# Cross attention: probabilities turned by VectorE in blocks of 32 by 32 and placed through DRAM, image sums two steps behind, text in a stage of its own

## The chip, the cores and the metric

The kernel runs on one core of a Trainium2 chip. The metric is the device time of one execution in microseconds, the median of three runs. A profile of one further execution gives the span and the rows below.

## The reference, cut to what matters

The program is a two-layer perceiver block: 16 batches of 64 latents of width 256 attend to a context of 1601 rows. The change is in the cross attention of the second layer (16 heads of 64, inner width 1024). Its keys and values have two parts: the first 77 context rows (text) with weights of their own, and the other 1524 (image). Each part has its own softmax, and the two results are added.

```python
def _attend(q, k, v):
    sim = jnp.einsum('bihd,bjhd->bhij', q, k) * SCALE
    attn = jax.nn.softmax(sim, axis=-1)
    out = jnp.einsum('bhij,bjhd->bihd', attn, v)
...
# text:  k = ctx[:, :77] @ Wk,     v = ctx[:, :77] @ Wv
# image: k = ctx[:, 77:] @ Wk_ip,  v = ctx[:, 77:] @ Wv_ip
# x = x + (attend(q, text) + attend(q, image)) @ Wo + bo
```

(The last three lines are a summary, with x normalised before it is projected to q.)

## The kernel before, in words

The program is a row of stages, each with its own block of engine programs: load, norm, positions, the first layer's local attention (near_attention or far_attention), self attention, a mixture of experts, then norm and cross_attention, a scan and a second mixture.

cross_attention goes over 8 tiles of 128 tokens (two batches each). A tile has 16 steps: 2 batches x 8 pairs of heads. A step handles one batch's 64 tokens for two heads, 128 rows of scores. Image keys and values are never formed: key_side multiplies the queries by the key weights (a, 128 x 256), scores multiplies a by the transposed context ct (3 x 508 columns), sums multiplies the turned probabilities by the context rows cn, and value_side applies the value weights to the turned result. Precision is kept by splitting: a, ct, cn and the turned probabilities are each held as a high part in fp32r and a low part (the rest), and three products are added.

In step n, TensorE does in this order: text scores of n (L2151); the twelve transposes of the probabilities of n - 1 (turn, L2169) into PSUM; the scores of n (18 matmuls, L2159 to L2161); the transpose of the text probabilities (L2176); the transpose of the sums of n - 2 (L2190); key_side for n + 1 (L2145); the sums of n - 1 (24 matmuls, L2182 of 512 columns and L2183 of 256); value_side of n - 2 (L2201, L2203). ScalarE copies the turned probabilities out of PSUM as high part (pt_hi, L2302), then does the exponentials of n (L2365 image, L2368 text). VectorE subtracts for the low part (pt_lo, L2308), takes the maxima of the scores (L2417, L2418), makes the bias (L2421), scales the text probabilities (L2410) and joins the two halves of the sums (L2432, L2435).

The text keys and values are made inside the steps, for the next tile or batch (L2127: keys, 3 uses of a PSUM bank per tile; L2136: values, 4 uses per tile). At tile borders TensorE also makes the queries (L2117) and the output projection (L2213). GpSimd splits the context, 8 pieces per batch (L1907, L1909), which SyncE loads one at a time into one buffer, staged (L1900, L2032). It runs ahead of the steps, as far as the two sets of buffers allow. The order on each engine is written out by hand; waits are on semaphores, and every engine runs its queue in order. The positions of the first layer go through DRAM: load_positions issues 32 small DMAs (L303) in near_attention.

## Time and profile before

| | |
|---|---|
| median of 3 runs | 2578.5 us (2574.81 to 2583.28) |
| the profiled execution | 2586.37 us, its span 2584.0 us |
| TensorE matmuls busy | 2328.9 us (90%), weight loads 1821.4 |
| VectorE, ScalarE, GpSimd busy | 1314.9 (51%), 957.4 (37%), 856.9 (33%) us |
| bytes moved | 141.32 MB, mean 55 GB/s |

The span is the time from the first to the last instruction in the trace; the profiled execution's own time is 2.4 us longer. An engine's busy time counts its own instructions alone, so a waiting engine shows as idle. A matmul's time in the trace overlaps the next one's, so its cost is read from the distance between starts.

### The profile page before, as it was taken

What the parts mean: (1) busy time and instruction counts of PE and PEld (TensorE: products, weight loads), DVE (VectorE), ACT (ScalarE), POOL (GpSimd) and SP (SyncE); (2) the same over time, 40 slices, a digit from 0 to 9 for tenths busy, and PEclk for the clock granted to TensorE, in tenths of its full rate; (3) what the DMA queues carried; (4) which work ended last, traced back from release to release, by engine and by line L of the source; (5) the groups of instructions that cost most, each with busy time, mean ns of one, the idle gap of its engine ahead of it and who ended that gap; (6) DMA issues with size and microseconds to landing.
All of it is one profiled execution on the core that took longest, in us unless ns stands there. A gap on an engine that the chain in (4) does not pass through costs nothing. (4 is left out here: it accounts for less than half of the span.)

```text
span 2584.0 us, 35941 instructions
## 1 busy us (share of the span) xinstructions
PE 2328.9 (90%) x13845; PEld 1821.4 (70%) x13845; DVE 1314.9 (51%) x2478; ACT 957.4 (37%) x2031; POOL 856.9 (33%) x534
## 2 busy tenths in 40 slices
PE   3787759949999999999999999999999998687896
PEld 2454445647888888888888888888888886234673
DVE  4897533344544544544544544544444444695543
ACT  2564121123443433443443443443343443452330
POOL 2563215225414314314224224233232100262444
PEclk8898869979999999999999999999999998798898
DMA  4100063122112102102002001111111003101372
GB/s 102 17 11 5 1 232 113 35 90 58 44 35 62 37 29 68 31 14 89 25 19 82 27 25 60 44 31 54 50 32 54 13 1 156 57 0 41 109 143 88
DMA packets 69927, 141.32 MB, mean 55 GB/s; under 512 B 24912, under 2 KB 42576, under 8 KB 65408
## 3 DMA queue, kind: packets, MB, share of 16 engines
q1 hardware_dynamic: 62992, 120.50, 14.8%
q0 software_dynamic: 6768, 18.49, 3.1%
q8 instruction: 117, 1.92, 0.3%
q14 instruction: 50, 0.41, 0.1%
HBM read 124.21 MB, written 14.75 MB: 54 GB/s over the span
## 5 line engine op out<-in xcount | busy, mean ns | idle before, releaser
L2182 PE MATMUL img_ps<-cn,pt_hi 127*128 127x512 f32 x1536 | 551.2, 400 | 10.4 <-POOL cn L1909 10.3
L2183 PE MATMUL img_ps<-cn,pt_lo 127*128 127x256 f32 x1536 | 430.0, 280 | 0.0
L1907 POOL TENSOR_SCALAR ct<-staged 128x762 fp32r<-128x762 f32 x64 | 136.1, 2127 | 755.5 <-DMA staged<-in_ctx_t 523.8
L2182 PEld LDWEIGHTS img_ps<-cn,pt_hi 127*128 127x128 f32 x1536 | 289.7, 189 | 70.2 <-POOL cn L1909 10.5
L2159 PE MATMUL s_ps<-ct,a_hi 128*128 128x508 f32 x768 | 312.3, 407 | 0.0
L2308 DVE TENSOR_TENSOR pt_lo<-t_ps,pt_hi 127x512 fp32r<-127x512 f32 x384 | 241.4, 684 | 135.1 <-ACT pt_hi L2302 135.1
L2161 PE MATMUL s_ps<-ct,a_lo 128*128 128x508 f32 x768 | 301.6, 393 | 0.0
L2160 PE MATMUL s_ps<-ct,a_hi 128*128 128x508 f32 x768 | 301.5, 393 | 0.0
L2183 PEld LDWEIGHTS img_ps<-cn,pt_lo 127*128 127x128 f32 x1536 | 289.4, 188 | 0.0
L2365 ACT ACTIVATE prob<-s_ps,bias 128x1524 f32<-128x1524 f32 x128 | 196.5, 1535 | 141.4 <-DVE bias L2421 141.4
L2302 ACT ACTIVATE pt_hi<-t_ps 127x512 fp32r<-127x512 f32 x384 | 202.0, 599 | 80.8 <-PE t_ps L2169 76.9
L2418 DVE TENSOR_REDUCE top<-s_ps 128x1 f32<-128x1524 f32 x128 | 222.0, 1735 | 0.0
L2432 DVE TENSOR_SCALAR o_part<-img_ps,inv 128x256 f32<-128x256 f32 x128 | 61.9, 484 | 307.1 <-PE img_ps L2183 307.1
L1907 POOL TENSOR_SCALAR cn<-staged 128x768 fp32r<-128x768 f32 x64 | 136.6, 2134 | 230.4 <-DMA staged<-in_ctx_n 183.1
L2332 ACT ACTIVATE pt_txt<-t_ps 77x128 f32<-77x128 f32 x128 | 34.9, 273 | 453.5 <-PE t_ps L2176 453.5
L2169 PE MATMUL t_ps<-small,prob 128*127 128x128 f32 x1536 | 196.9, 278 | 0.0
L2417 DVE TENSOR_REDUCE top<-s_ps 128x1 f32<-128x77 f32 x128 | 30.4, 238 | 321.9 <-PE s_ps L2161 321.9
L2169 PEld LDWEIGHTS t_ps<-small,prob 128*127 128x127 f32 x1536 | 180.7, 191 | 0.1
L2161 PEld LDWEIGHTS s_ps<-ct,a_lo 128*128 128x128 f32 x768 | 144.7, 188 | 31.9
L2160 PEld LDWEIGHTS s_ps<-ct,a_hi 128*128 128x128 f32 x768 | 145.6, 190 | 27.4
L2159 PEld LDWEIGHTS s_ps<-ct,a_hi 128*128 128x128 f32 x768 | 144.9, 189 | 27.2
L1632 PE MATMUL up_ps_b<-up_all_m,xt_b 128*128 x436 | 152.9, 483 | 1.5 <-issue 0.8
(369 smaller groups left out, 3929.4 us busy)
## 6 DMA issues: line engine op xcount, KB each, us to landing
staged<-in_ctx_n SPq DMA_DIRECT2D x64, 384.0 KB, 3.1
staged<-in_ctx_t SPq DMA_DIRECT2D x64, 381.0 KB, 3.2
up_all_m<-in_up SPq DMA_DIRECT2D x8, 2048.0 KB, 13.0
down_all_m<-in_down SPq DMA_DIRECT2D x8, 1024.0 KB, 27.1
sums_m<-y_b SPq DMA_DIRECT2D x63, 128.0 KB
w_shared<-in_wq SPq DMA_DIRECT2D x7, 1024.0 KB, 5.5
w_shared<-in_wo SPq DMA_DIRECT2D x7, 1024.0 KB, 4.9
win<-in_ctx_near SPq DMA_DIRECT2D x16, 128.0 KB, 2.0
```

Source lines behind the costliest of these rows:

```text
L1632: last = nc.tensor.matmul(up_ps[j % 2][:, own], xt[j % 2][:, c, :], m.up[:, bass.ds(expert, 1), c, own].rearrange("p a h -> p (a h)"), sta ...
L1907: nc.gpsimd.tensor_scalar(hi, piece, 1.0, None, ALU.mult).then_inc(first.hi_done, 1)
L2159: nc.tensor.matmul(out, a_hi[:, c, :], ct[b][:, 0, c, cols], start=c == 0, stop=False)
L2160: nc.tensor.matmul(out, a_hi[:, c, :], ct[b][:, 1, c, cols], start=False, stop=False)
L2161: last = nc.tensor.matmul(out, a_lo[:, c, :], ct[b][:, 0, c, cols], start=False, stop=c == C - 1)
L2169: last = nc.tensor.transpose(t_ps[bank][0:IBLK, j * P:(j + 1) * P], prob[:, at:at + IBLK], k.ident)
L2182: nc.tensor.matmul(img_ps[:], pt_hi[0:IBLK, j, :], rows[0:IBLK, :, j, :], start=j == 0, stop=False)
L2183: last = nc.tensor.matmul(img_ps[:, D:2 * D], pt_lo[0:IBLK, j, :], rows[0:IBLK, 0, j, :], start=False, stop=j == IB - 1)
L2302: nc.scalar.activation(out, t_ps[bank][0:rows, 0:cols], ACT.Copy).then_inc(hi_kept, 1)
L2308: nc.vector.tensor_tensor(out, t_ps[bank][0:rows, 0:cols], hi.bitcast(F32), ALU.subtract).then_inc(t_kept[bank], 1)
L2365: nc.scalar.activation(prob[:, TXT:M].rearrange("p (j m) -> p j m", j=SB), s_ps[:, 1:4, 0:SBLK], ACT.Exp, bias=bias[s][:, 1:2], scale=SCAL ...
L2418: nc.vector.tensor_reduce(top[s][:, 1:2], s_ps[:, 1:4, 0:SBLK], mybir.AxisListType.XY, ALU.max).then_inc(topped, 1)
```

## The change

The twelve transposes of a step leave TensorE. VectorE turns the image probabilities in blocks of 32 by 32, in four instructions (128 x 384) as soon as the image exponential is done. SyncE stores each result (192 KB) to DRAM and, when it has landed, loads it back into 32 partitions in the order that the sums need: four stores and four loads a step. ScalarE and VectorE split what came back (moved, in SBUF) into pt_hi and pt_lo in two halves of 128 x 768 each, where before they read PSUM in three parts of 127 x 512. The sums run two steps behind the scores instead of one, in blocks of 128 context rows instead of 127, as 36 matmuls of 256 columns into one half of the bank, so that VectorE needs one instruction on the sums instead of two. One context piece is loaded in each step, behind the step's eight DMAs. The loops over tiles are unrolled.

text_stage, new, stands between the positions stage and the local attention: it makes all text keys (24 uses of a bank) and values (20 uses), stores them to DRAM, and cross_attention loads them tile by tile. load_positions moves into it from near_attention and far_attention.

```diff
+            load_positions(sp, k)
+            for p in range(PAIRS1):
+                wait_kept(sp, len(K_COLS) * (p + 1))
+                sp.dma_start(k.k_txt[:, :, p, :].rearrange("i q n -> q i n"),
+                             keys[p % KEYS][:].rearrange("q (i n) -> q i n", i=NT)).then_inc(keys_out[p % KEYS], 16)
...
+                for c in range(C):
+                    if kind == "k":
+                        last = nc.tensor.matmul(out[:, 0:cols.stop - cols.start], w.wk[:, c, at * P:(at + 1) * P],
+                                                w.text[:, c, cols], start=c == 0, stop=c == C - 1)
+                    else:
+                        last = nc.tensor.matmul(out[0:rows_of(at), :], w.text[:, c, at * P:at * P + rows_of(at)],
+                                                w.wv[:, c, cols], start=c == 0, stop=c == C - 1)
+                last.then_inc(done, 1)
...
-        load_positions(sp, k)
...
-        prob = sb("prob1", [P, M])
+        prob = sb("prob1", [P, TXT + IB * P])
+        blocks = sb("prob_blocks", [P, Q, IB, QR])
+        block_rows = nc.dram_tensor("prob_rows", (2, Q, P, RUN), F32).ap()
+        moved = [sb(f"prob_moved{s}", [P, Q, IB, QR]) for s in range(2)]
...
+            for g in range(N):
+                s, (i, b, p, n) = g % 2, parts(g)
+                if g >= 2:
+                    sp.wait_ge(moved_in[s], 16 * Q * (g // 2))
+                for m in range(Q):
+                    sp.wait_ge(turned, Q * g + m + 1)
+                    sp.dma_start(block_rows[s, m], blocks[:, m].rearrange("p j r -> p (j r)")).then_inc(stored[m], 16)
+                if g >= 2:
+                    sp.wait_ge(split_done, 2 * (g - 1))
+                for m in range(Q):
+                    sp.wait_ge(stored[m], 16 * (g + 1))
+                    sp.dma_start(moved[s][m * QR:(m + 1) * QR].rearrange("c a j r -> c a (j r)"),
+                                 block_rows[s, m].rearrange("(a c) f -> c a f", a=Q)).then_inc(moved_in[s], 16)
+                if g // PAIRS1 + 1 < NB:
+                    load(g // PAIRS1 + 1, g % PAIRS1)
...
-            def sums(n):
-                rows = cn[n // PAIRS1]
-                for j in range(IB):
-                    nc.tensor.matmul(img_ps[:], pt_hi[0:IBLK, j, :], rows[0:IBLK, :, j, :], start=j == 0, stop=False)
-                    last = nc.tensor.matmul(img_ps[:, D:2 * D], pt_lo[0:IBLK, j, :], rows[0:IBLK, 0, j, :],
-                                            start=False, stop=j == IB - 1)
-                last.then_inc(summed, 1)
+            def sums(g):
+                rows = cn[g // PAIRS1 % 2]
+                if g % PAIRS1 == 0:
+                    pe.wait_ge(cn_split, 4 * (g // PAIRS1) + 4)
+                if g:
+                    pe.wait_ge(sums_kept, g)
+                for h in range(2):
+                    pe.wait_ge(split_done, 2 * g + h + 1)
+                    for j in range(IB)[half(h)]:
+                        n = min(P, IMG - j * P)
+                        for at, (left, right) in enumerate(((pt_hi, 0), (pt_hi, 1), (pt_lo, 0))):
+                            last = nc.tensor.matmul(img_ps[:, 0:D], left[0:n, j, :], rows[0:n, right, j, :],
+                                                    start=j == 0 and at == 0, stop=j == IB - 1 and at == 2)
...
+            for g in range(N + 3):
+                if g < N:
+                    if g:
+                        pe.wait_ge(exp_done, g)
+                    kept(a_place)
+                    text_scores(g)
+                    scores(g)
+                if 1 <= g <= N:
+                    turn_text(g - 1)
+                if g >= 3:
...
+                if 2 <= g <= N + 1:
+                    sums(g - 2)
...
+                if 1 <= g <= N:
+                    act.wait_ge(moved_in[(g - 1) % 2], 16 * Q * ((g - 1) // 2 + 1))
+                    for h in range(2):
+                        if g >= 2:
+                            act.wait_ge(summed if h else half_summed, g - 1)
+                        nc.scalar.activation(in_quarters(pt_hi, h), by_block(moved[(g - 1) % 2], h),
+                                             ACT.Copy).then_inc(pt_hi_kept, 1)
...
+                    dve.wait_ge(image_exp, g + 1)
+                    source = prob[:, TXT:].rearrange("p (j m c) -> p m j c", j=IB, m=Q)
+                    for m in range(Q):
+                        if g:
+                            dve.wait_ge(stored[m], 16 * g)
+                        nc.vector.transpose(blocks[:, m], source[:, m]).then_inc(turned, 1)
...
+                if 1 <= g <= N:
+                    for h in range(2):
+                        dve.wait_ge(pt_hi_kept, 2 * (g - 1) + h + 1)
+                        nc.vector.tensor_tensor(in_quarters(pt_lo, h), by_block(moved[(g - 1) % 2], h),
+                                                in_quarters(pt_hi, h).bitcast(F32), ALU.subtract).then_inc(split_done, 1)
+                if 2 <= g <= N + 1:
+                    dve.wait_ge(summed, g - 1)
+                    nc.vector.tensor_scalar(o[:], img_ps[:, 0:D], inv[(g - 2) % 3][:, 1:2], None,
+                                            ALU.mult).then_inc(sums_kept, 1)
```

## Rows read from the trace of the kernel before

**Rows 1.** Busy time in stretches: length, us and (instructions) per engine, TensorE's clock, DMA share, GB/s.
```profile
1442.73:1454.06 11.33, 11.33 (x79) 9.76 (x75) 5.57 (x12) 4.71 (x11) 0.00 (x0) 1.00 0.00 1
595.27:2143.60 1548.33, 1545.74 (x10164) 1317.39 (x10164) 742.92 (x1400) 625.87 (x1440) 466.83 (x239) 1.00 0.14 41
```
**Rows 2.** Timeline of an ordinary step on TensorE: start us, duration us.
```profile
1442.75 0.45 PE L2151 MATMUL s_ps<-k_txt,q 128*128 128x77 f32 x2
1443.03 1.54 PE L2169 MATMUL t_ps<-small,prob 128*127 128x128 f32 x12
1444.32 0.47 PE L2159 MATMUL s_ps<-ct,a_hi 128*128 128x508 f32 x1
...
1448.54 0.27 PE L2176 MATMUL t_ps<-small,prob 128*77 128x128 f32 x1
...
1449.23 0.48 PE L2182 MATMUL img_ps<-cn,pt_hi 127*128 127x512 f32 x1
...
1453.37 0.28 PE L2183 MATMUL img_ps<-cn,pt_lo 127*128 127x256 f32 x1
...
1454.08 0.45 PE L2151 MATMUL s_ps<-k_txt,q 128*128 128x77 f32 x2
```
**Rows 3.** Timeline of the same step on VectorE and ScalarE.
```profile
1450.67 0.17 DVE L2421 TENSOR_SCALAR bias<-top 128x2 f32<-128x2 f32 x1
...
1450.87 1.53 ACT L2365 ACTIVATE prob<-s_ps,bias 128x1524 f32<-128x1524 f32 x1 [0.97 <-DVE bias L2421]
...
1452.60 0.20 ACT L2368 ACTIVATION_READ_ACCUMULATOR prob<-s_ps,bias 128x1 f32 x1
```
**Rows 4.** The page's costliest groups: busy us, mean ns of one, idle before.
```profile
L2308 DVE TENSOR_TENSOR pt_lo<-t_ps,pt_hi 127x512 fp32r<-127x512 f32 x384 | 241.4, 684 | 135.1 <-ACT pt_hi L2302 135.1
...
L2302 ACT ACTIVATE pt_hi<-t_ps 127x512 fp32r<-127x512 f32 x384 | 202.0, 599 | 80.8 <-PE t_ps L2169 76.9
```
**Rows 5.** Single lines of the code: duration ns min/median/max, first and last start us.
```profile
L739 DVE TENSOR_TENSOR share<-tent,marks x32: 1214/1484/1755, 69.4 to 241.3; 128x1536 f32<-128x1536 f32 x16, 128x1024 f32<-128x1024 f32 x16
...
L2421 DVE TENSOR_SCALAR bias<-top x128: 169/170/1553, 567.1 to 2151.8; 128x2 f32<-128x2 f32 x128
...
L2410 DVE TENSOR_SCALAR prob<-prob,inv x128: 261/264/1894, 569.5 to 2155.4; 128x77 f32<-128x77 f32 x128
...
L1907 POOL TENSOR_SCALAR cn<-staged x64: 2127/2134/2192, 561.1 to 2017.7; 128x768 fp32r<-128x768 f32 x64
```
**Rows 6.** Timeline of SyncE's queue: two DMAs issued one after the other.
```profile
40.82 0.81 SPq L345 DMA_DIRECT2D pos_rows<-where  x2
```
**Rows 7.** DMA queue (packets, MB, share of 16 engines) and issues (KB, us to landing).
```profile
q1 hardware_dynamic: 62992, 120.50, 14.8%
...
staged<-in_ctx_n SPq DMA_DIRECT2D x64, 384.0 KB, 3.1
...
pos_rows<-where SPq DMA_DIRECT2D x1, 280.0 KB, 2.7
```
**Rows 8.** The sixteen stores of L163, 128 KB each to DRAM: time to landing.
```profile
DMA to landing us min/median/max: 1.7/4.9/9.3
```
**Rows 9.** Timeline of TensorE: text keys of a tile; a step with one values use.
```profile
554.71 4.37 PE L2127 MATMUL t_ps<-text,wk_txt 128*128 128x154 f32 x32
...
1501.06 0.34 PE L2151 MATMUL s_ps<-k_txt,q 128*128 128x77 f32 x2
...
1514.06 0.34 PE L2151 MATMUL s_ps<-k_txt,q 128*128 128x77 f32 x2
```
**Rows 10.** Busy time at the start of the local attention, columns as in rows 1.
```profile
46.00:54.00 8.00, 5.05 (x46) 4.13 (x47) 1.39 (x2) 0.62 (x2) 1.95 (x2) 0.64 0.26 40
```
**Rows 11.** GpSimd's L603 in the local attention: what ended its waits (us, times).
```profile
DMA pos<-pos_rows: 14.5, 2
```
**Rows 12.** Timeline: batch 0's last context piece on GpSimd; the last step's sums.
```profile
585.87 1.80 POOL L1909 TENSOR_TENSOR cn<-staged,cn 128x768 fp32r<-128x768 f32 x1
...
2158.03 0.50 PE L2182 MATMUL img_ps<-cn,pt_hi 127*128 127x512 f32 x1
```

More of the change, by code:

```diff
@@ L2022, in _, with boundary, projects, half @@
+        def boundary(g):
+            return g % STEPS == STEPS - 1 and g < N - 1
+        def projects(g):
+            return g // STEPS - 1 if g % STEPS == 2 and g >= STEPS else None
+        def half(h):
+            return slice(h * IB // 2, (h + 1) * IB // 2)
         @block.sync
         def _(sp):
-            def load(i, b, pieces):
-                for j in pieces:
-                    wait_split(i, b, j)
-                    if j < 4:
-                        load_ct(sp, first, src["ctx_t"][i * 2 + b], j)
-                    else:
-                        blocks = slice((j - 4) * CNB, (j - 3) * CNB)
-                        sp.dma_start(staged[:].rearrange("p (j d) -> p j d", d=D),
-                                     src["ctx_n"][i * 2 + b][:, blocks, :]).then_inc(piece_in, 16)
@@ L2068, in _, with load_keys @@
-            load(NT - 1, 1, range(8))
+                    sp.wait_ge(cn_split, 4 * b + j - 4)
+                if j < 4:
+                    load_ct(sp, first, src["ctx_t"][b], j)
+                else:
+                    rows = slice((j - 4) * CNB, (j - 3) * CNB)
+                    sp.dma_start(staged[:].rearrange("p (j d) -> p j d", d=D),
+                                 src["ctx_n"][b][:, rows, :]).then_inc(piece_in, 16)
+            def load_keys(i, part):
+                heads = slice(part * PAIRS1 // 2, (part + 1) * PAIRS1 // 2)
+                sp.dma_start(k_txt[:, heads].rearrange("p j b m -> p j (b m)"), k.k_txt[i][:, heads]).then_inc(k_in, 16)
@@ L2087, in _ @@
-            split(0, 1)
+                        rows = slice((j - 4) * CNB, (j - 3) * CNB)
+                        hi, lo = (cn[b % 2][:, part, rows, :].rearrange("p j d -> p (j d)") for part in range(2))
+                        split_piece(nc, pool, first, staged[:], hi, lo, 8 * b + j, cn_split)
+            nc.gpsimd.memset(prob[:, TXT + IMG:], 0.0).then_inc(pad_zeroed, 1)
+            split(0, range(4, 8))
+            split(1)
             nc.gpsimd.tensor_tensor(k.x[:], k.x[:], k.bo1[:].unsqueeze(1).broadcast_to([P, NT, D]),
@@ L2089, in _, with use @@
                                     ALU.add).then_inc(bo_added, 1)
-            for i in range(1, NT):
-                for b in range(2):
-                    split(i, b)
+            for b in range(2, NB):
+                split(b)
         @block.tensor
         def _(pe):
-            def use(ring, split=False):
-                bank, count = ring.next(split)
-                if not isinstance(count, int) or count > 1:
+            ring = Ring()
+            def use():
+                bank, count = ring.next()
+                if count > 1:
@@ L2147, in key_side, with text_scores @@
                 last.then_inc(t_done[bank], 1)
[L2149 to L2150 removed]
+                return ring.place(1)
+            def text_scores(g):
+                i, b, p, n = parts(g)
+                if n in (0, 4):
+                    pe.wait_ge(k_in, 32 * i + (16 if n and i else 32 if not i else 16) + (16 if n and i else 0))
                 nc.tensor.matmul(s_ps[:, 0, 0:TXT], q[:, p, b].rearrange("p r n -> p (r n)"), k_txt[:, p, b, :],
                                  start=True, stop=True)
[L2154 to L2162 removed]
@@ L2317, in keep_queries @@
         def keep_queries(eng, copy, mine, ring):
-            for half in range(2):
+            for side in range(2):
                 bank, count = ring.next()
-                if half == mine:
+                if side == mine:
                     eng.wait_ge(t_done[bank], count)
@@ L2825, in load_local @@
                         sp.dma_start(buffer[:], src[name]).then_inc(loaded, 16)
+                    text.load(sp)
                 load_stage(nc, k, src)
```

622 lines of the change are left out of this document (292 added, 330 removed).

## The prediction

> **What bounds the kernel now.** I read the summary of busy time first, then the busy time by stretch, then the timeline of one step of the cross attention, engine by engine, then the landing times of the DMAs. The cross attention runs 128 steps. From the third step to the last it takes 1548.33 us, 60% of the 2584.0 us span, TensorE busy in 1545.74 of them at the full granted clock of 1.00, i.e. 2.4 GHz [rows 1]. An ordinary step takes 11.33 us: TensorE is busy in all of it, VectorE in 5.57 and ScalarE in 4.71 [rows 1, 2]. So this stage is worth what TensorE's instruction stream is worth, as long as nothing else becomes longer than it.
>
> I put time zero of a step at the transpose of the text probabilities, 1448.54. Seen from there [rows 2]: the sums start at 0.69 and the last of their 24 matmuls at 4.83, the next step's text scores at 5.54, the twelve transposes at 5.82, the scores at 7.11, and the next zero is 11.33. The reader is to see two pitches: 12 transposes with their 12 weight loads in 1.29 us (0.107 each), and 24 sum matmuls in 4.14 to 4.25 us. VectorE and ScalarE in the same frame [rows 3]: the maxima are done when the bias starts at 2.13, the exponential of the image part runs 2.33 to 3.86, the text part's accumulator is read by 4.26. TensorE needs that at 5.54, so the softmax chain has 1.28 us to spare.
>
> **The change, part by part.**
>
> *TensorE, each step.* Removed: the twelve transposes, 1.29 us [rows 2]. The sums go from 12 x (512 + 256) columns to 36 x 256, the same columns. Would 36 weight loads instead of 24 cost? A load for a 512-column matmul now happens under a 256-column one of about 0.115 us, and transposes take a new load every 0.107 us [rows 2], so a load each 0.115 us is already shown: nothing. If it did not hold, 12 more exposed loads of about 0.1 us would take the whole gain back; that is the price, and the rows speak against it. A new wait in the middle of the sums: 0 to 0.2 us, I take 0.1. New step: 11.33 - 1.29 + 0.10 = 10.14 us.
>
> *VectorE, each step.* It loses three subtractions of 0.684 us from PSUM [rows 4] and one of the two steps on the sums (0.48), and gets four 32 by 32 transposes of 384 elements and two subtractions of 768 elements with both inputs in SBUF. VectorE with two SBUF inputs takes 1.21 us for 1024 and 1.75 for 1536 elements [rows 5], so 768 take 0.95. No row shows a transpose. Lower bound: the 0.684 us for 512 elements scaled, 0.5 us; upper bound the slowest rate per element in the trace, GpSimd's 2.13 us for 768 [rows 5], 1.07 us. I take 0.5: all of VectorE's rows lie at about one element per nanosecond. In the frame: transposes from 3.95 to 5.95, reciprocal and text factor to 6.4, subtractions to 8.3, the factor on the sums to 8.8. The next maxima are due at 10.14 + 0.2, the sums turned at 10.25. Slack 1.45 us. ScalarE: two copies of 768 elements, 0.9 us each at most (0.599 for 512 [rows 4]), after 4.26, done by 6.1; the subtractions follow them. It fits.
>
> *The way through DRAM.* SyncE issues a DMA in about 0.43 us (two in 0.81 [rows 6]), with the wait 0.48. 192 KB land in 2.3 us: between 2.7 for a store of 280 KB and 3.1 for a load of 384 KB, shrunk by size, and the lowest store of 1.7 [rows 7, 8]. Stores issued at 4.5, 5.0, 5.5 and 6.0, the first landed at 6.8, loads issued 6.8 to 8.25, the last landed at 10.6. ScalarE asks for it in the next step after 4.26, at 14.4; being late there by another 2 us would still not reach the sums, which are two steps behind. So the round trip is hidden with about 4 us. Bytes: 1.57 MB a step more; the hardware queue moved 120.50 MB in 14.8% of the 16 engines' 2584 us, i.e. 315 GB/s [rows 7], so 5.0 us, and 1.2 for the context piece: 6.2 of 10.1 us. Behind SyncE's waits stand the context piece (one a step now, eight are needed in eight steps) and the weights wo and wq; all of these are due steps later.
>
> *Text.* In the loop a use for values costs 13.00 - 11.33 = 1.67 us and the keys of a tile 4.37 [rows 2, 9]. Between third and last step: 30 x 1.67 + 7 x 4.37 = 80.7; the difference to 125 ordinary steps and the stretch, with the queries and projections that stay, allows 78. I take 78. The new stage does the same key columns (8 x 4.37 = 35 us) and 20 uses of values instead of 32 (33.4), 68.4 us at full clock; the granted clock around its place is 0.64 over the first 8 us [rows 10], +3; entering, last copy, last store of 2.3 us and leaving, 5.5: 77 us. GpSimd waits 14.5 us there for the positions [rows 11], which now land under the text stage; 10 us of it come back (0 to 14).
>
> *Start and end.* The fourth context piece ends at 587.67 [rows 12] and holds the first sums: now in step 1, which makes step 2 start at 595.27. After, the first sums stand in step 2. SyncE issues this piece's load at about 580.4 (585.87 less 2.2 for the piece's first instruction and 3.3 for landing) and only then the first step's stores: landed 583, loads landed 587, copies and subtraction to 589, sums to 593, so step 3 starts at about 594. The end: the last sums start 4.7 us after the last image exponential (2158.03 [rows 12] against 2143.6 + 9.65, the ordinary step's distance from its text scores); now transposes 2.0, last store 2.4, load 2.3, copy and subtraction 1.8 make 8.5, but the step before is 1.3 shorter: +2.5.
>
> *Sum.* Third step's start to last step's start: 1548.6 before. After, from step 3: 124 x 10.14 + 54.2 (queries and projections, 1548.6 - 125 x 11.33 - 78) = 1311.6, and 1.3 us earlier: -238. Ends +2.5, text stage +77, positions -10: -169. For the lock below 15: -154. The profiled execution took 2586.37 us around its 2584.0 span, so 2432 by it; the median of the runs is 2578.5, so **2425 us**.
>
> **A rule weighed.** VectorE's factor of the bias takes 0.170 us in the median and up to 1.553, that on the text probabilities 0.264 and up to 1.894 [rows 5], while GpSimd's instructions on the pieces take 2.13 and 1.80 us [rows 5, 12]. Such a short instruction that grows by nearly one of GpSimd's looks like it waits for it. The Trainium skill says so, in "SBUF — State Buffer", section Who interferes with whom: one of the two holds the shared ports for its whole instruction and the other fully blocks, and it counts VectorE instructions with two SBUF inputs among those concerned. By that rule the trace agrees for the short ones; for the two subtractions, which read PSUM before and SBUF after, no row here tells, and by it they would wait too.
>
> **The rivals.**
>
> *B, GpSimd's pieces block VectorE (20%).* A piece is issued at 8.7 and lands in 3.1 us or a little more, so GpSimd starts at 1.7 to 2.6 of the next step, in each step, where before it had free steps [rows 1, 7]. If it starts before 2.13, the bias waits up to 2.1 us: the softmax chain's 1.28 us are used up, +0.8 us. If it starts after 3.6, the text factor or the subtractions wait past VectorE's slack, +0.3 to 1. Between the two it costs nothing. +0.3 to +1.1 us x 124: 2455 to 2550, 2490 in the middle. For it: that the times lie so near; against it: a late start pushes the next piece to another phase.
>
> *C, SyncE's queue (5%).* Each step waits in order for the first store. The cycle is a store's landing plus about 2.6 us for loads and piece, so from 7.6 us landing on it sets the step. Stores did land in up to 9.3 us, median 4.9 [rows 8], but behind large weight loads. At 8.5 the step is 11.1: 2530.
>
> *D, slower: VectorE's own queue (8%).* If a transpose takes 1.07 us, VectorE's chain ends at 11.1 and it becomes the bound; with one block by GpSimd of 1 us in each step the step is 12.0. Without the steps' gain the change is worth -11.3 (one step less before the steady state) - 1.3 - 78 + 2.5 + 77 - 10 = -21, so it turns slower from a step of 11.50 us on. At 12.0: 2640.
>
> *E, better (5%).* No wait in the sums, no block, 14 us of positions: 124 x 0.10 + 15 + 4 less, about 2393, and below with a shorter text stage. *F, even (2%)*: a step of about 11.5.
>
> **How the numbers follow.** The forecast's case has 60%, 2388 to 2455. Below 2388 lie about 4%; above 2535 lie D's 8%, half of C and a tenth or so of B, together 12 to 14%. The range is 2388 to 2535. A difference under 0.3% (8 us) can't be told from none: its chance is 2%; slower has 9% (D and a part of C), faster 89%.
>
> **What would show it.** An ordinary step of 10.1 us between two text scores, TensorE without idle time. 36 sum matmuls at 0.115 us. VectorE's transposes at about 0.5 us. The copies of the turned probabilities never waiting for DMAs. The bias and the subtractions at their lowest times in most steps. A text stage of 77 us. Wrong would make it: transposes twice as long, subtractions of 2 us and more, waits of the text scores for the exponential or of turning the sums for VectorE, a lower granted clock.

## Result and profile after

The changed kernel takes 2439.07 us in the median of 4 runs (2435.73 to 2441.9), the kernel before 2576.84 in 4 runs beside them: a ratio of 0.9461, 95% interval 0.9438 to 0.9484, 138 us faster. Predicted were 2425 us, range 2388 to 2535. The profiled execution took 2435.73 us around a span of 2433.6; predicted for it were 2432.

That 2432 came so near is partly luck, as two rows show. The first work behind the cross attention is the statistics of the next normalization; the first row is of the kernel before, the second of the changed one (fewest, median and most ns, then first and last start):

```profile
L174 DVE BATCH_NORM_STATS2 stats_e<-x_sb x8: 410/412/429, 2170.4 to 2172.7; 128x6 f32<-128x256 f32 x8
```

```profile
L175 DVE BATCH_NORM_STATS2 stats_e<-x_sb x8: 408/408/428, 2034.6 to 2036.9; 128x6 f32<-128x256 f32 x8
```

From there to the end of the span it is 2584.0 - 2170.4 = 413.6 us before and 2433.6 - 2034.6 = 399.0 after, in code that the change does not touch. In the profiles of the twelve experiments below this stretch takes 399 to 401 us in the four of the second set and 410 to 417 in the eight of the first and third, whatever was edited, and the kernel before takes 2576.0 us beside the second set, 2589.8 and 2588.9 beside the others. The two profiles keep step to within 1 us through 374 us of this stretch; what is left takes 39.0 us before and 25.1 after. So 14.6 us between the two profiles are not the change's, and experiments are compared by their ratio to the kernel before beside them, or by stretches of the cross attention. In ratios my forecast was 2432 / 2586.4 = 0.9403 and the result 0.9461: the gain was overestimated by 15 us.

The stretch of the cross attention by windows, answering to [rows 1]: the fourth to the last step, then the first three (length, busy us and instructions of PE, PEld, DVE, ACT and POOL, granted clock, DMA share, GB/s):

```profile
665.53:2000.72 1335.19, 1313.21 (x9751) 1186.88 (x9749) 973.21 (x1643) 580.32 (x1255) 486.91 (x239) 0.99 0.69 199
624.12:665.53 41.41, 25.60 (x110) 21.55 (x111) 18.50 (x28) 10.53 (x21) 19.76 (x10) 0.79 0.50 136
```

124 steps take 1335.19 us. One ordinary step, answering to [rows 2, 3], all engines in order of time (start, length; SPq is the DMA queue that SyncE feeds):

```profile
717.74 1.81 DVE L2478 TENSOR_TENSOR pt_lo<-prob_moved,pt_hi 128x768 fp32r<-128x768 f32 x2
...
719.47 0.47 DVE L2482 TENSOR_SCALAR o<-img_ps,pairs 128x256 f32<-128x256 f32 x1
...
720.50 0.27 PE L2257 MATMUL t_ps<-small,prob 128*77 128x128 f32 x1
...
721.19 0.48 PE L2271 MATMUL img_ps<-cn,pt_hi 128*128 128x256 f32 x2
...
722.62 0.17 DVE L2453 TENSOR_SCALAR pairs<-pairs 128x2 f32<-128x2 f32 x1
...
722.83 1.53 ACT L2402 ACTIVATE prob<-s_ps,pairs 128x1524 f32<-128x1524 f32 x1 [0.97 <-DVE pairs L2453]
...
723.61 2.13 POOL L2001 TENSOR_SCALAR cn<-staged 128x768 fp32r<-128x768 f32 x1 [5.85 <-DMA staged<-in_ctx_n]
...
724.48 1.96 DVE L2466 STREAM_TRANSPOSE prob_blocks<-prob 128x384 f32<-128x384 f32 x4 [1.36 <-ACT prob L2402]
...
724.65 0.84 ACT L2414 ACTIVATE pt_hi<-prob_moved 128x768 fp32r<-128x768 f32 x1
...
725.13 1.81 SPq L2147 DMA_DIRECT2D prob_rows<-prob_blocks  x4
...
725.43 0.28 PE L2271 MATMUL img_ps<-cn,pt_lo 116*128 116x256 f32 x1
...
726.13 0.45 PE L2237 MATMUL s_ps<-k_txt,q 128*128 128x77 f32 x2
...
726.52 1.21 DVE L2470 TENSOR_SCALAR prob<-prob,pairs 128x77 f32<-128x77 f32 x1
...
727.08 1.83 SPq L2152 DMA_DIRECT2D prob_moved<-prob_rows  x4
```

My zero, the transpose of the text probabilities, is at 720.50, and the next at 730.59: 10.09 us. The sums run from 0.69 to 4.93 without a gap in their middle, then come the next text scores at 5.63. The bias is at 2.12 and the exponential from 2.33 as before; the four transposes take 1.96 us from 3.98, each copy of 768 elements 0.84, two subtractions 1.81. The stores are issued at 4.63, the loads at 6.58. GpSimd's piece starts at 3.11, and the text factor at 726.52 takes 1.21 instead of 0.26 us. VectorE still ends in time: in the step before, with such a factor too, it was free from 719.94 and needed at 720.70.

The landing times (count, KB, median us from issue to landing), answering to [rows 7, 8]:

```profile
prob_rows<-prob_blocks SPq DMA_DIRECT2D x512, 192.0 KB, 2.1
prob_moved<-prob_rows SPq DMA_DIRECT2D x512, 192.0 KB, 3.6
...
w_shared<-in_wo SPq DMA_DIRECT2D x7, 1024.0 KB, 7.5
```

### The profile page after: what moved, and what is told of

It is laid out like the page before. It is cut to its first block and busy times, and to the rows that moved or that the text cites. A ratio compares the mean times of both kernels' runs of the same rounds, so it can differ in the third digit from the quotient of the medians.

```text
span 2433.6 us, 37422 instructions
## 1 busy us (share of the span) xinstructions
PE 2160.2 (89%) x13637; PEld 1726.1 (71%) x13637; DVE 1570.4 (65%) x2756; ACT 925.0 (38%) x1869; POOL 877.5 (36%) x535
## 3 DMA queue, kind: packets, MB, share of 16 engines
q8 instruction: 115, 1.88, 0.3%
## 5 line engine op out<-in xcount | busy, mean ns | idle before, releaser
L2271 PE MATMUL img_ps<-cn,pt_hi 128*128 128x256 f32 (+1 forms) x3072 | 569.7, 287 | 3.0 <-DVE pt_lo L2478 3.0
L2271 PEld LDWEIGHTS img_ps<-cn,pt_hi 128*128 128x128 f32 (+1 forms) x3072 | 477.3, 191 | 3.2 <-issue 3.2
L2271 PE MATMUL img_ps<-cn,pt_lo 128*128 128x256 f32 (+1 forms) x1536 | 435.9, 284 | 0.0
L2466 DVE STREAM_TRANSPOSE prob_blocks<-prob 128x384 f32<-128x384 f32 x512 | 250.6, 547 | 183.8 <-ACT prob L2402 175.9
L2271 PEld LDWEIGHTS img_ps<-cn,pt_lo 128*128 128x128 f32 (+1 forms) x1536 | 292.6, 190 | 0.0
L2478 DVE TENSOR_TENSOR pt_lo<-prob_moved,pt_hi 128x768 fp32r<-128x768 f32 x256 | 277.9, 1124 | 9.4 <-ACT pt_hi L2414 9.2
L2402 ACT ACTIVATE prob<-s_ps,pairs 128x1524 f32<-128x1524 f32 x128 | 196.5, 1535 | 136.7 <-DVE pairs L2453 136.7
L2414 ACT ACTIVATE pt_hi<-prob_moved 128x768 fp32r<-128x768 f32 x256 | 214.7, 842 | 62.7 <-PE img_ps L2271 46.7
L2450 DVE TENSOR_REDUCE pairs<-s_ps 128x1 f32<-128x1524 f32 x128 | 222.0, 1735 | 0.0
L2003 POOL TENSOR_TENSOR cn<-staged,cn 128x768 fp32r<-128x768 f32 x64 | 125.6, 1963 | 5.3
## 6 DMA issues: line engine op xcount, KB each, us to landing
up_all_m<-in_up SPq DMA_DIRECT2D x8, 2048.0 KB, 12.8
```

The costliest lines, as they stand in the source:

```text
L2003: nc.gpsimd.tensor_tensor(lo, piece, hi.bitcast(F32), ALU.subtract).then_inc(done, 1)
L2271: last = nc.tensor.matmul(img_ps[:, 0:D], left[0:n, j, :], rows[0:n, right, j, :], start=j == 0 and at == 0, stop=j == IB - 1 and at == 2)
L2402: nc.scalar.activation(prob[:, TXT:M].rearrange("p (j m) -> p j m", j=SB), s_ps[:, 1:4, 0:SBLK], ACT.Exp, bias=bias[g % 2][:, 1:2], scale= ...
L2414: nc.scalar.activation(in_quarters(pt_hi, h), by_block(moved[(g - 1) % 2], h), ACT.Copy).then_inc(pt_hi_kept, 1)
L2450: nc.vector.tensor_reduce(top[g % 2][:, 1:2], s_ps[:, 1:4, 0:SBLK], mybir.AxisListType.XY, ALU.max).then_inc(topped, 1)
L2466: nc.vector.transpose(blocks[:, m], source[:, m]).then_inc(turned, 1)
```

## The experiments

Three sets of four, timed beside 8 or 9 runs of the kernel before. "Loop" is the stretch from the fourth to the last step's text scores in the profile (1335.2 us in the changed kernel).

**The text part alone.** The new text stage and early positions with the old `cross_attention`, from which the text uses are taken out:

```
+            load_keys(0, 0)
+            load_keys(0, 1)
...
-            for part in range(K_USES):
-                text_keys(start, part)
```

> Only the text part of the change: the text stage and the early positions, with the old probabilities (twelve transposes on TensorE, sums one step behind) in the loop. My theory: the loop loses about 78 us of text work, the stage costs 75 and the positions and the first keys give back about 11, so 2562 us (2550 to 2570) where before is 2577; steps of 11.32 us at every n, with a border step of about 15. Rival: the text part carries more of the gain than this, because text work sat at places where TensorE waited anyway or because the stage is paid less than it looks: below 2540 us.

Measured: 0.9964 (0.9938 to 0.9989), about 9 us less, or 2568 at 2577 for before. The text half is worth little, as expected; of the 138 us some 129 belong to the probabilities. Ordinary steps are 11.33 us again, the border steps 15.6. Two things were smaller than I thought: from the third step to the last 70 us went where I had 78 (4 us of the difference are two longer steps, 14.0 and 12.85 us, so the text itself was 74), and TensorE waits 15.8 us at the start for the last context piece.

**The transposes back on TensorE.**

```
                 if g:
                     pe.wait_ge(sums_kept, g)
+                for j in range(IB):
+                    nc.tensor.transpose(img_ps[:, D:D + P], k.ident, k.ident)
```

> The changed kernel with twelve more 128 by 128 transposes on TensorE in each step (of a constant, into a part of the bank that nobody reads), just ahead of the sums. My theory: TensorE's stream alone sets the step, so each step grows by 1.29 us to 11.4 and the whole by 128 x 1.29 = 165 us, to 2604 us (2590 to 2612). Rival: another engine or the way through DRAM is already close to setting the step, and part of the 1.29 us falls into waits: below 2560 us.

Measured: 1.0073 (1.005 to 1.0095), 0.0612 more than the changed kernel, 158 us at 2577. The ordinary step is 11.41 us instead of 10.10. All of the 1.3 us appear in the step, so TensorE's stream alone sets it; how much room the other engines have this run does not tell.

**GpSimd's split left out.**

```
+                    if b >= 2:
+                        pool.wait_ge(piece_in, 16 * (8 * b + j) + 16)
+                        pool.sem_inc(ct_split if j < 4 else cn_split, 1)
-                    if j < 4:
+                    elif j < 4:
```

> The changed kernel with GpSimd's split of the context left out from the third sample on (the pieces are still loaded, the first two samples' halves are used again), so its output is not the reference's. My theory: what GpSimd takes from VectorE in an ordinary step lies in VectorE's slack; only the tile borders get shorter, by up to 1.5 us where the text factor was held up, and the stall behind the bias addition stays: 2428 to 2437 us, ordinary steps still 10.1. Rival B of the prediction: the pieces cost 0.3 to 1.1 us in each step, so 40 to 135 us go: 2305 to 2400 us.

Measured: 0.9466 (0.9447 to 0.9486), no difference; loop 1332.9 us, 2.3 less, though one projecting step of 17.63 us (14.41 in the changed kernel) takes 3.2 of what the others give; ordinary steps 10.10. Rival B's price is out: in ordinary steps the pieces cost nothing. My own expectation for the borders was wrong too: all seven stay at 15.6 us with the same last wait of up to 1.9 us, so the pieces add 0.3 us to them on average (15.93 in the changed kernel) and something else makes them.

**Every transpose twice.**

```
+                        nc.vector.transpose(blocks[:, m], source[:, m]).then_inc(turned_before, 1)
+                    dve.wait_ge(turned_before, Q * g + Q)
+                    for m in range(Q):
                         nc.vector.transpose(blocks[:, m], source[:, m]).then_inc(turned, 1)
```

> The changed kernel with VectorE's four transposes done twice in each step, which is rival D's price of 1.07 us a transpose. The trace shows VectorE idle for 0.85 us before its maxima in a step where a piece held up its text factor by 1.2 us, and 1.9 us in one without: with 2.02 us more its cycle is 10.2 without a piece in its way and 11.3 with one. My theory: 0.1 to 1.15 us a step, 2452 to 2583 us, about 2510 with a piece in the way of every second step, and waits of TensorE for the exponential. Rival: VectorE is only 65% busy, so the added 2 us disappear: 2439 to 2445 us.

Measured: 0.9844 (0.9809 to 0.9879), 0.0383 more, 99 us; loop 1431.2 us, ordinary steps between 10.0 and 12.1, mean 10.7. Of the 96 us that the loop is longer the ordinary steps have 65; the borders (17.6 to 18.1 us) have 14 more, the projecting steps 9 and the steps behind the borders, six of seven at the lower clock at first, 7. The size was as expected, the wait was not the one I named. The row gives TensorE's waits by what ended them (total us, times, longest):

```profile
PE t_ps L2280 <- DVE o L2486: 66.7, 89, 1.9
```

TensorE waits for `o`, the scaled sums, VectorE's last work in a step, and not for the exponential. That is VectorE's nearest due time: the next step wants `o` 0.1 us after its zero.

**Another order at the tile borders.** Where a tile ends, the changed kernel's engines do this (ScalarE, VectorE and TensorE, in order of time):

```profile
1662.71 1.96 DVE L2466 STREAM_TRANSPOSE prob_blocks<-prob 128x384 f32<-128x384 f32 x4 [1.69 <-ACT prob L2402]
...
1664.75 1.49 DVE L2470 TENSOR_SCALAR prob<-prob,pairs 128x77 f32<-128x77 f32 x1
...
1666.16 1.38 DVE L2430 COPY q<-t_ps 64x512 f32<-64x512 f32 x2
...
1667.57 1.83 DVE L2478 TENSOR_TENSOR pt_lo<-prob_moved,pt_hi 128x768 fp32r<-128x768 f32 x2
...
1667.64 0.68 PE L2228 MATMUL t_ps<-q,wk 128*128 128x128 f32 x4 [0.58 <-issue]
...
1668.36 0.38 ACT L2386 ACTIVATE a_hi<-t_ps 128x256 fp32r<-128x256 f32 x1 [0.42 <-PE t_ps L2228]
...
1669.43 0.48 DVE L2482 TENSOR_SCALAR o<-img_ps,pairs 128x256 f32<-128x256 f32 x1
1669.83 0.41 DVE L2437 TENSOR_TENSOR a_lo<-t_ps,a_hi 128x256 fp32r<-128x256 f32 x1
...
1670.35 0.65 PE L2237 MATMUL s_ps<-k_txt,q 128*128 128x77 f32 x2 [1.53 <-issue]
```

TensorE turns the key side only when VectorE has kept the new queries (ended 1667.54), behind a text factor of 1.49 us; then `a_lo` stands behind two subtractions and `o` and ends at 1670.24, and the text scores start at 1670.35 after 1.53 us of waiting. The granted clock then (columns as in the first table):

```profile
1668.00:1671.00 3.00, 1.47 (x18) 1.25 (x18) 2.22 (x4) 0.61 (x2) 0.00 (x0) 0.90 1.01 246
1671.00:1673.50 2.50, 2.50 (x8) 1.95 (x8) 0.00 (x0) 0.00 (x0) 1.64 (x1) 0.50 0.00 1
```

After waits of 0.58 and 1.53 us it is 0.50, the lower of the two levels (1.2 GHz), for the 2.5 us of the second line and 3.4 in all. It came behind three of the seven borders (after waits of 0.60 and 1.53 us, of 0.58 and 1.53, and of 1.88 alone), and the step behind these takes 12.95, 11.65 and 11.64 us instead of 10.1. Behind the other four, with waits of the same sizes, the clock stayed at 1.00. The experiment's additions (the same calls leave their old places behind the copies and the subtractions):

```
                 if boundary(g):
                     keep_queries(act, copy, 0, ring)
+                    keep_a(g + 1)
...
+                    if boundary(g):
+                        keep_queries(dve, copy, 1, ring)
+                        dve.sem_inc(queried, 1)
                     dve.wait_ge(exp_done, g + 1)
...
+                if boundary(g):
+                    keep_a_lo(g + 1)
                 if 1 <= g <= N:
                     for h in range(2):
                         dve.wait_ge(pt_hi_kept, 2 * (g - 1) + h + 1)
```

> The changed kernel with another order at the tile borders alone: ScalarE copies the high half of the next tile's first key side before the turned probabilities, VectorE the new queries before the text factor and the low half before the subtractions. My theory: the border steps are 1.5 to 2 us longer than their work because these two small copies stand behind 2 to 3 us of other work; they go from 15.6 - 16.2 to about 14.3 us, 7 times, and the low clock in the step behind some of them goes too (1.5 to 2.9 us, up to three times): 10 to 18 us less, a ratio to before of 0.939 to 0.942 where the changed kernel has 0.946. Rival: GpSimd's pieces or the queries' copies themselves set the border, and the time stays within 3 us.

Measured: 0.9408 (0.9385 to 0.943), 0.0053 less, 14 us; loop 1318.9, 16.3 us shorter. A border in it, VectorE and then TensorE:

```profile
1659.67 1.35 DVE L2429 COPY q<-t_ps 64x512 f32<-64x512 f32 x2
...
1663.05 0.42 DVE L2436 TENSOR_TENSOR a_lo<-t_ps,a_hi 128x256 fp32r<-128x256 f32 x1 [0.72 <-ACT a_hi L2386]
```

```profile
1661.98 0.61 PE L2228 MATMUL t_ps<-q,wk 128*128 128x128 f32 x4
...
1663.57 0.42 PE L2237 MATMUL s_ps<-k_txt,q 128*128 128x77 f32 x2 [0.48 <-issue]
```

The last wait is 0.48 us, all seven borders take 14.2 to 14.3 us and the steps behind them 10.1. The theory holds, the low clock included: in this kernel and the two of three and four edits below, which have the same order, none of 21 borders is followed by it.

**The bias addition in eight.** In the changed kernel one step of the first tile takes 15.41 us: TensorE waits 3.58 us in it and then has the lower clock for 3.5 us. GpSimd, VectorE and TensorE there:

```profile
727.62 4.59 POOL L2193 TENSOR_TENSOR x_sb<-x_sb,bo 128x2048 f32<-128x2048 f32 x1
727.65 6.25 DVE L2478 TENSOR_TENSOR pt_lo<-prob_moved,pt_hi 128x768 fp32r<-128x768 f32 x2
...
734.44 0.41 PE L2279 MATMUL t_ps<-small,o 128*128 128x128 f32 x2 [3.58 <-DVE o L2482]
```

```
-            nc.gpsimd.tensor_tensor(k.x[:], k.x[:], k.bo1[:].unsqueeze(1).broadcast_to([P, NT, D]),
-                                    ALU.add).then_inc(bo_added, 1)
+            for t in range(NT):
+                added = nc.gpsimd.tensor_tensor(k.x[:, t, :], k.x[:, t, :], k.bo1[:], ALU.add)
+            added.then_inc(bo_added, 1)
```

> The changed kernel with GpSimd's one addition of the output bias (4.59 us over 128 x 2048) cut into eight of 128 x 256. My theory: VectorE's subtraction with both inputs in SBUF waits for the end of a GpSimd instruction, so the step at 726 us with its 5.38 us subtraction and 15.41 us goes back to about 10.1; the other steps stay: 5 us less, a ratio of 0.944. Rival: the long subtraction waits for something else there (the copy of the high half, a semaphore, the whole series), and the step stays at 15 us or so.

Measured: 0.9467 (0.9446 to 0.9488), no difference in the whole; the 5 us expected are 0.002 of the time, no more than the interval's half width. The step itself goes from 15.41 to 10.75 us. In this profile it is taken back by one projecting step of 19.8 us instead of 14.4 (ScalarE waits 3.08 us for blocks there, ahead of a small copy, as in the next experiments), and by borders and steps at the low clock, which are 3.5 us longer together. GpSimd and VectorE in the shortened step:

```profile
728.78 7.03 POOL L2194 TENSOR_TENSOR x_sb<-x_sb,bo 128x256 f32<-128x256 f32 x8
```

```profile
728.80 2.95 DVE L2479 TENSOR_TENSOR pt_lo<-prob_moved,pt_hi 128x768 fp32r<-128x768 f32 x2
```

The two subtractions take 2.95 us together instead of 6.25: VectorE gets in between two of GpSimd's instructions. So the long subtraction did wait for GpSimd's instruction to end.

**The loads held back.**

```
+                sp.wait_ge(scored, min(g + 2, N))
                 for m in range(Q):
                     sp.wait_ge(stored[m], 16 * (g + 1))
```

> The changed kernel with the four loads of each step's blocks held until TensorE has ended the next step's scores, 3.3 us later than now (from 6.8 us after my zero of a step to 10.1). My theory: the way through DRAM had about 4 us to spare and two more beyond; the time stays within 5 us, a ratio of 0.944 to 0.949, ScalarE's copies wait up to 1 us in some steps. Rival C: the queue or the landing is near the limit: a step grows by 0.3 to 1 us, 40 to 125 us more, a ratio of 0.96 to 0.995.

Measured: 0.9684 (0.9655 to 0.9713), 0.0223 more, 57 us. Neither theory had the place. Most ordinary steps stay at 10.1 to 10.5 us, but the seven projecting steps take 17 to 21 us, 19.3 on average instead of 14.4: 34 of the 45 us that the loop is longer in this profile, which is of the fastest of the four executions. ScalarE and TensorE in one of them:

```profile
1729.84 1.58 ACT L2415 ACTIVATE pt_hi<-prob_moved 128x768 fp32r<-128x768 f32 x2 [4.73 <-DMA prob_moved<-prob_rows]
1731.32 0.20 ACT L2380 ACTIVATE head_out<-t_ps 128x64 f32<-128x64 f32 x1
```

```profile
1731.58 5.89 PE L2308 MATMUL t_ps<-w_shared,head_out 128*128 128x128 f32 x32 [4.98 <-ACT head_out L2380]
```

The projection wants the heads' output of this step at once; ScalarE's copy of it stands behind `pt_hi`, which waits 4.73 us for the blocks.

**The same, with this copy ahead of the wait in the projecting steps.**

```
+                if projects(g) is not None:
+                    keep_head(g)
                 if 1 <= g <= N:
                     act.wait_ge(moved_in[(g - 1) % 2], 16 * Q * ((g - 1) // 2 + 1))
...
-                if g >= 3:
+                if g >= 3 and projects(g) is None:
+                    keep_head(g)
```

> The loads held until the end of the next step's scores, as in the run before, and ScalarE's copy of the heads' output moved ahead of its copies of the turned probabilities in the eight steps that project. My theory after that run: its 55 us came almost wholly through this copy, which stands behind ScalarE's wait for the blocks, and from smaller waits at the borders; so the projecting steps go from 17 - 21 back to 14.2 us and the ratio from 0.968 to 0.948 - 0.956. Rival: late blocks reach the sums themselves, or the output weights land late: the projecting steps stay at 17 to 21 us and the ratio above 0.964.

Measured: 0.9534 (0.9514 to 0.9554), 0.0150 less than without it, 39 us; the projecting steps take 14.47 us, which gives back 34 us. Between the two profiles the loop is only 21 us shorter, since other steps grew. 19 us over the changed kernel remain: late `o` (22.6 us of TensorE's waits), borders of up to 17.3 us and, in each tile, a ninth step of 10.5 to 14.6 us.

**Later still.** The wait is for `exp_done` instead of `scored`.

> The same freed kernel with the loads held until the next step's exponentials are done, 7.5 us later than in the changed kernel. My theory: the last block lands at about 19.7 us after my zero, its copies and subtractions end at 22 where the sums want the first half at 20.8: ordinary steps grow by 0.5 to 1.2 us, a ratio of 0.97 to 1.0. Rival: two steps of distance hide this as well, and the ratio stays under 0.96.

Measured: 1.1304 (1.1269 to 1.1339); ordinary steps 14.1 us on average. I expected 0.5 to 1.2 us a step and got 4. VectorE in one step, then TensorE's largest wait:

```profile
1506.74 2.45 DVE L2484 TENSOR_TENSOR pt_lo<-prob_moved,pt_hi 128x768 fp32r<-128x768 f32 x2 [6.05 <-ACT pt_hi L2423]
1509.12 0.47 DVE L2488 TENSOR_SCALAR o<-img_ps,pairs 128x256 f32<-128x256 f32 x1
```

```profile
PE t_ps L2280 <- DVE o L2488: 321.3, 114, 5.9
```

The loop's windows row:

```profile
667.37:2473.36 1805.99, 1456.55 (x9750) 1302.46 (x9749) 943.54 (x1640) 576.09 (x1253) 530.32 (x239) 0.91 0.52 147
```

The subtractions of the step's blocks end at 1509.2, and only then comes `o`, though its sums had ended before 1502. The sums do have two steps of distance; `o` and the heads' output, which belong to older steps and are due at once, stand behind them in the engines' order. The waits for `o` are 321 of the 471 us that the loop is longer. Another part is the low clock that follows such waits: 0.91 is granted on average over the loop, 0.99 in the changed kernel; the two were not taken apart. The true slack of the blocks is that of `o`: it ends at 719.94 in the step shown above and is wanted at 720.61.

**The sums in their old form.**

```
-                        for at, (left, right) in enumerate(((pt_hi, 0), (pt_hi, 1), (pt_lo, 0))):
-                            last = nc.tensor.matmul(img_ps[:, 0:D], left[0:n, j, :], rows[0:n, right, j, :],
...
+                        nc.tensor.matmul(img_ps[:], pt_hi[0:n, j, :], rows[0:n, :, j, :], start=j == 0, stop=False)
+                        last = nc.tensor.matmul(img_ps[:, D:2 * D], pt_lo[0:n, j, :], rows[0:n, 0, j, :],
...
```

> The changed kernel with the sums in the old form, 12 x (512 + 256) columns with 24 weight loads instead of 36 x 256 with 36; VectorE then takes only the first half of the result, so the product of the context's low halves is left out of the output. My theory: a weight load is hidden under 256 columns, and no more than the 0.1 us between the two forms in the profiles is in it: 0 to 13 us less, a ratio of 0.941 to 0.947. Rival: the twelve added loads are partly exposed, up to 0.1 us each: down to 150 us less, a ratio near 0.89.

Measured: 0.9423 (0.9404 to 0.9442), 0.0038 less, 10 us; ordinary steps 10.04 instead of 10.10. Twelve more matmuls with their weight loads, for the same columns, cost 0.07 us a step, 0.006 each; the rival's 0.1 each is out.

**Three and four edits together.** The border order and the bias in eight, and at the start the first stores between the context pieces:

> The changed kernel with the border order, the bias addition in eight, and the first step's stores and loads placed between the last three context pieces instead of behind them. My theory: the three act in different steps and add up: 10 to 18, 5 and 2 to 4 us less, together 17 to 27, a ratio of 0.9355 to 0.939. Rival: what one removes another gives back (the start is held by the context pieces alone, which now come later): 5 us less or no difference to the border order alone.

Measured: 0.9389 (0.9369 to 0.9409), 19 us less than the changed kernel as expected, but only 5 less than the border order alone, which is within the intervals; that the other two edits add is seen in the steps and not in the time. The borders are 14.24, the step with the bias 10.73; the first three steps take 36.9 instead of 41.4 us, but 2.7 of this come back in the fourth (12.8 us), whose blocks waited behind the last piece's issue. So the fourth version issues from the second step on one piece less ahead of the stores, and moves the heads' copy as above:

```
-                if g // PAIRS1 + 1 < NB:
-                    load(g // PAIRS1 + 1, g % PAIRS1)
+                if g == 0:
+                    load(0, 7)
+                if g and (g - 1) // PAIRS1 + 1 < NB:
+                    load((g - 1) // PAIRS1 + 1, (g - 1) % PAIRS1)
```

> The changed kernel with the border order, the bias addition in eight, the heads' copy ahead of the wait for the blocks in the projecting steps, and at the start a context piece less ahead of each of the first steps' stores. My theory: against the version with three of these the start gives 3 to 5 us (the third and fourth step together from 28.5 to about 24.6 us) and the projecting steps 2 to 5 us (all at 14.2): a ratio of 0.9345 to 0.9375. Rival: the start stays, because the last context piece alone sets it, and the projecting steps already were at their work: 0.9385 to 0.9395.

Measured: 0.9349 (0.9329 to 0.9368), 29 us less than the changed kernel, 168 less than the one before at 2577. The third and fourth step take 25.8 us, not 24.6, the projecting ones 14.18. The fourth to the last step:

```profile
662.75:1973.73 1310.98, 1304.79 (x9750) 1180.37 (x9748) 976.74 (x1637) 577.67 (x1254) 487.82 (x247) 1.00 0.71 202
```

1310.98 us with TensorE busy in 1304.79: what is left there is nearly all its own work.

## Why the prediction held, and where it was off

The terms of the sum against the profiled execution, in us:

| term | predicted | measured | off |
|---|---|---|---|
| start of the cross attention (560.54 before; text +77, positions -10) | 627.5 | 624.1 | -3.4 |
| its first three steps | 33.5 | 41.4 | +7.9 |
| 124 ordinary steps | 1257.4 (10.14) | 1253.0 (10.105) | -4.4 |
| queries, projections and single stalls | 54.2 | 82.2 | +28.0 |
| allowance for the lock | 15 | in the row above | -15.0 |
| last step's start to the next stage | 29.1 | 33.9 | +4.8 |
| the kernel behind it | 413.6 | 399.0 | -14.6 |
| span | 2430.3 | 2433.6 | +3.3 |

*TensorE's step* was right: 11.33 - 1.29 leaves 10.04, and the kernel with 24 sum matmuls has it. The 0.1 us that I put on a wait in the middle of the sums is not one; 0.07 of it come with the twelve additional matmuls and their weight loads, which I had at nothing. That the transposes set the gain is shown by putting them back.

*VectorE's chain* was right, and its one unknown price too: four transposes in 1.96 us, the subtractions 0.949 us in the median, the copies 0.843. With the transposes that was partly luck: no row had one, and 0.5 was the lower of two bounds for it. The reason given, one element per nanosecond, would make it 0.38; it is 0.49. The slack of 1.45 us was about right: 2 us more cost 0.6 us a step on average. So the place of rival D is real, and the forecast depended on the transposes' price; D's step of 12.0 us was too dear: with each transpose done twice, about 1.0 us for the two, it is 10.7.

*The way through DRAM* was right in its result and wrong in its reason. Stores land in 2.1 us where I had 2.3, loads in 3.6 instead of 2.3, the weights `wo` in 7.5 instead of 4.9, the DMA engines are busy in 0.69 of the stretch where I had 6.2 of 10.1. The blocks are still there when ScalarE asks, in all steps of the loop but one, where it waits 1.2 us. But "being late there by another 2 us would still not reach the sums" was the wrong question: it reaches `o` and the heads' output, as the three kernels with held loads show.

*Text.* The stage lasts 75.0 us from 45.86 to GpSimd's first instruction of the next at 120.81 (predicted 77), its keys and values as sized:

```profile
L526 PE MATMUL text_ps<-text_all,wk_txt 128*128 128x462 f32 (+1 forms) x96 | 35.1, 528 | 0.5 <-PEq L312 0.5
L529 PE MATMUL text_ps<-wv_txt,text_all 128*128 128x512 f32 (+1 forms) x80 | 34.8, 593 | 1.0 <-ACT text_values L549 1.0
...
L545 DVE COPY text_values<-text_ps 128x512 f32<-128x512 f32 (+1 forms) x10 | 6.9, 691 | 26.3 <-DMA v_txt_rows<-text_values 18.2 <-PE text_ps L529 8.1
```

The values' copies waited for the DMAs of earlier ones, which stood behind the key rows, yet TensorE lost only 1.0 us by it. The stage's start and the positions come to -11.4 instead of -10. The loop lost 74 of my 78 us by the text-alone kernel (70 and its two longer steps). I had not worked out the 78; the 4 us too many made the 54.2 us for queries and projections, which are the rest of a difference, 4 us too few.

*The start* was mis-sized by 7.9 us:

```profile
632.58 15.28 SPq L2124 DMA_DIRECT2D staged<-in_ctx_n  x3
647.90 1.98 SPq L2147 DMA_DIRECT2D prob_rows<-prob_blocks  x4
651.72 1.77 SPq L2152 DMA_DIRECT2D prob_moved<-prob_rows  x4
```

```profile
657.38 1.58 ACT L2414 ACTIVATE pt_hi<-prob_moved 128x768 fp32r<-128x768 f32 x2 [11.81 <-DMA prob_moved<-prob_rows]
```

(SyncE's queue, then ScalarE.) SyncE's first stores are issued at 647.90, behind the last three context pieces, although VectorE had begun to turn at 634.3; the loads follow their landing, and ScalarE waits 11.81 us. My step let SyncE issue the last piece and then the stores, but took the piece's time from the old kernel, 19.9 us after the first text scores; here the three are issued until 23.7 us after them.

*The specials*, the queries and projections that my sum carries over unchanged as 54.2 us, are the step that failed: they are 82.2. Over ordinary steps, the seven borders cost 5.83 us each where the text-alone kernel has 4.29, so 10.8 us more; steps at the low clock behind them 5.9; the bias addition 5.3; the projections 1.5 more; and 4 are the text's, as said. I had carried them over as TensorE's work without reading what the new order of VectorE and ScalarE puts ahead of their small copies. The border experiment shows this cause by removing it. My allowance of 15 us for the lock covered half of this, partly by chance: the lock's own share is the bias addition's 5.3 us and what the pieces cost the loop, 2.3 us by the kernel without the split, or 5.5 without that one's long projecting step.

*The end* costs 7.3 us where I had 2.5 (ScalarE, then TensorE):

```profile
2017.29 0.85 ACT L2414 ACTIVATE pt_hi<-prob_moved 128x768 fp32r<-128x768 f32 x1 [2.73 <-DMA prob_moved<-prob_rows]
```

```profile
2020.83 0.41 PE L2279 MATMUL t_ps<-small,o 128*128 128x128 f32 x2 [1.92 <-DVE o L2482]
...
2022.28 0.63 PE L2271 MATMUL img_ps<-cn,pt_hi 128*128 128x256 f32 x2
```

The last blocks cost a wait of 2.73 us, and two series of sums follow the last scores instead of one, the second delayed by `o` and at the low clock (0.63 us for a pair of matmuls where an ordinary step has 0.40).

*The rule weighed.* A row shows the lock where I had looked for it and harder: a subtraction with both inputs in SBUF took 5.38 us instead of 0.949 while GpSimd's 4.59 us addition ran, and 1.5 us on average in the same place once that addition was cut in eight. It holds beside the ordinary pieces too: 31 of 256 subtractions take over 1.1 us, up to 2.61 apart from that one, and 79 of 128 text factors over 0.4; with GpSimd's split left out 2 and 7 do. By the rule of the Trainium skill, "SBUF — State Buffer", section Who interferes with whom, a VectorE instruction with two SBUF inputs contends with a GpSimd instruction that reads SBUF, and the trace agrees. Whether it matters is a question of slack: in ordinary steps most pieces came at 3 to 5.5 us after my zero, where they met the text factor (0.684 us in the median, 0.264 before) and, the later ones, a subtraction. That is 120 us of VectorE's time in all 128 steps, and outside the bias addition and the borders the slack took it. Of rival B there was the mechanism and not the price (by its own 0.3 to 1.1 us a step, counted as in rival C, its range was 2447 to 2546, not 2455 to 2550); rivals C, D and E did not come about.

## What to carry to other kernels

In an ordinary step, giving an engine's work to others pays what leaves the bounding engine's stream, if each small copy that it waits for still comes in time; so look at the exceptional steps (tile borders, projections, start, end) in the new order of each engine, not only at the ordinary one. A pipeline distance of two steps gives slack only to the instruction that is two steps away: in an in-order queue the older work behind it sets the true due time. Small copies that release the bounding engine belong ahead of long ones and ahead of waits for a DMA.

## What the hardware showed that I had not expected

- TensorE's waits at the seven borders were about 1.5 us after one of 0.58 to 0.72, or 1.88 to 1.93 us at once. Three of the seven were followed by the lower granted clock, for 3.4 to 6.9 us, at a cost of 1.5 to 2.9 us; the four others kept the full clock. With a single wait of 0.48 us (three kernels) or 0.64 us (the text-alone kernel) none of 28 borders was followed by it.
- One long GpSimd instruction held up VectorE for nearly its whole length: a subtraction with 0.949 us of work that started 0.03 us behind a GpSimd addition of 4.59 us took 5.38 us and ended 0.8 us after it.
- Loads of 192 KB into 32 partitions landed in 3.6 us, stores of the same 192 KB from 128 partitions in 2.1. Which of direction, partitions and traffic makes the difference was not tried.
- The stretch behind the cross attention took 399 to 401 us or 410 to 417 us by set of runs, and each set ran on a chip of its own. The difference lies in the last 40 us of the kernel: from 20 to 10 us before its end the granted clock is 0.50 in all profiles with the long form and 1.00 in all with the short one. What sets this was not tried.
